# A graph network on one core: f32 tables split into three bfloat16 parts by ScalarE and VectorE in turns

## What is computed

```python
src = jnp.concatenate([_s, _d, _loop]); dst = jnp.concatenate([_d, _s, _loop])   # 103125 edges

# layer 0: attention with a bias by edge type
scores = jnp.sum(q[dst] * (k[src] + rel_bias), axis=-1) / SCALE
...
out = jax.ops.segment_sum(attn[:, :, None] * v[src], dst, num_segments=n)

# layer 1: three times
h = (x @ W).reshape(n, H, D)
e = jax.nn.leaky_relu(e_src[src] + e_dst[dst], NEG_SLOPE)
alpha = w / (denom[dst] + 1e-16)                     # w = exp(e - max)
out = jax.ops.segment_sum(h[src] * alpha[:, :, None], dst, num_segments=n)
```

## Time and profile before

| | us |
|---|---|
| runs | 8020.83, 8024.5, 8024.66 |
| median | 8024.5 |
| profiled execution | 8015.14 |
| its span | 8013.4 |

### The profile page before, as it was taken

How to read it: one execution, slowest core, us unless ns; L and a number is a source line. 1 busy time by engine, 2 the same in 40 slices (tenths; PEclk the granted TensorE clock), 3 DMA queues, 4 the chain that set the end, 5 groups by cost and what they waited for, 6 DMA issues and landing times. The chain is left out here.

```text
span 8013.4 us, 112882 instructions
## 1 busy us (share of the span) xinstructions
PE 2909.3 (36%) x28649; PEld 2368.4 (30%) x28650; DVE 4677.0 (58%) x10839; ACT 1435.1 (18%) x3773; POOL 3668.7 (46%) x4402
## 2 busy tenths in 40 slices
PE   4189633455555523344223432345200000001344
PEld 3168512344444422243223431334200000000122
DVE  9677345566666646687567764677544444444333
ACT  0123100111111112222112221344311111110000
POOL 0155224443333324565445544544466666563655
PEclk9999986676777766677566765666655555555677
DMA  0034223344434423345334443334332231222334
GB/s 21 10 92 108 58 75 96 96 105 101 101 88 96 92 59 70 80 83 77 67 75 83 84 69 64 77 74 73 53 51 51 52 52 51 49 51 55 77 83 80
DMA packets 293996, 576.70 MB, mean 72 GB/s; under 512 B 137262, under 2 KB 182043, under 8 KB 273827
## 3 DMA queue, kind: packets, MB, share of 16 engines
q0 software_dynamic: 113232, 255.82, 21.2%
q1 hardware_dynamic: 142642, 278.18, 11.3%
q10 hardware_dynamic: 38049, 41.86, 1.7%
HBM read 479.10 MB, written 29.32 MB: 63 GB/s over the span
## 5 line engine op out<-in xcount | busy, mean ns | idle before, releaser
L2992 PE MATMUL bank<-tab,oh 128*128 128x136 bf16 x11700 | 906.9, 251 | 704.3 <-PEq L2984 383.6
L2992 PEld LDWEIGHTS bank<-tab,oh 128*128 128x128 bf16 x11700 | 876.7, 113 | 765.2 <-issue 765.2
L1422 PE MATMUL bank<-ident,hid 128*128 128x128 f32 x125 | 55.8, 446 | 2622.7 <-PEq L1421 1482.1
L1422 PEld LDWEIGHTS bank<-ident,hid 128*128 128x128 f32 x125 | 22.7, 181 | 2669.4 <-issue 2669.4
L2735 POOL DMA_INDIRECT land_a<-table,idx_a x624 | 653.5, 1047 | 228.4 <-issue 166.4
L2754 POOL DMA_INDIRECT land_r<-table,idx_r x492 | 507.5, 1031 | 215.5 <-issue 148.4
L2915 ACT ACTIVATE rows<-bank 128x408 f32<-128x408 f32 x936 | 398.0, 514 | 848.6 <-ACTq L2914 640.2
L2841 DVE TENSOR_TENSOR prod<-prod 128x128 f32<-128x128 f32 (+4 forms) x621 | 536.5, 864 | 14.6
L2571 PE MATMUL bank<-tab_l,oh_l 128*128 128x128 bf16 x3846 | 407.5, 241 | 222.1 <-PEq L2534 102.0
L2827 DVE TENSOR_TENSOR prod<-rows,bank 128x5376 f32<-128x5376 f32 x75 | 431.6, 5755 | 61.1 <-DVEq L2826 30.5
L3218 PE MATMUL bank<-tab_l,oh_l 128*128 128x384 bf16 x1250 | 263.8, 381 | 454.9 <-PEq L3212 333.3
(11 more groups left out here) (515 smaller groups left out, 8530.2 us busy)
## 6 DMA issues: line engine op xcount, KB each, us to landing
loc<-el_loc SPq DMA_DIRECT2D x78, 1088.0 KB
loc_l<-el_loc SPq DMA_DIRECT2D x52, 1088.0 KB
typ_l<-el_typ SPq DMA_DIRECT2D x52, 672.0 KB
rows_r<-land_r SPq DMA_DIRECT2D x123, 272.0 KB
landings_l<-landings_l SPq DMA_DIRECT2D x41, 784.0 KB
attr<-in_edge_attr ACTq DMA_DIRECT2D x75, 343.8 KB
land_a<-table,idx_a POOLq DMA_INDIRECT x936
land_r<-table,idx_r POOLq DMA_INDIRECT x492
```

What stands on the lines that cost most here:

```text
L2992: last = pe.matmul(got[g % full][:, (c - of[0]) * W1:(c - of[0] + 1) * W1], oh[:, o], tab[:, t, x], start=n == 0, stop=n == len(parts) - 1 ...
```

## The change

The five steps of a group are divided. ScalarE makes the high part (`act_high`) and the middle part (`act_middle`) with activation copies; VectorE makes the two subtractions (`split_rest`, `split_low`), of which the second writes the low part straight as bfloat16, so the last cast goes. They hand on through `high_ready`, `rest_ready` and `middle_ready`. `rest` has two buffers, which in the attention and convolution passes lie in `kp` and `prod`, tensors that are unused at this time; `whole` has three. VectorE subtracts group g + 1 ahead of the low part of group g. ScalarE's order is the high parts of groups 0, 1, 2, the middle parts of 0 and 1, and then one high part (two groups ahead) and one middle part (one group ahead) at each step n.

In `l0_pass` ScalarE's `take_landed(0)` moves between step 3 and step 4. In `conv_pass` each step stands ahead of the copy of bank n. `sum_pass` gets a ScalarE program, with these copies alone. The diff, cut to one of three alike copies of each part (line numbers of the kernel before):

```diff
@@ -2089 @@  l0_pass
-            whole = [spare[:, k * BANKC * W0:...] for k in range(2)]
-            rest = spare[:, 2 * BANKC * W0:3 * BANKC * W0].rearrange("p (t w) -> p t w", w=W0)
+            whole = [spare[:, k * BANKC * W0:...] for k in range(3)]
+            rest = [kp[:].rearrange("p c w -> p (c w)")[:, k * BANKC * W0:...] for k in range(2)]
...
+            def act_high(act, g):
+                act.wait_ge(s(f"whole_in{g % 3}"), 16)
+                act.sem_inc(s(f"whole_in{g % 3}"), -16)
+                act.activation(tab_of(g)[:, :, 0], whole_of(g), ACT.Copy).then_inc(s("high_ready"), 1)
+
+            def act_middle(act, g):
+                act.wait_ge(s("rest_ready"), 1)
+                act.sem_inc(s("rest_ready"), -1)
+                act.activation(tab_of(g)[:, :, 1], rest_of(g), ACT.Copy).then_inc(s("middle_ready"), 1)
+
+            def act_split(act, n):
+                for g in range(n + 2 if n else 0, min(n + 3, len(tiles))):
+                    act_high(act, g)
+                for g in range(n + 1 if n else 0, min(n + 2, len(tiles))):
+                    act_middle(act, g)
...
-                        sp.wait_ge(s(f"whole_free{g % 2}"), 1)
+                        sp.wait_ge(s(f"whole_free{g % 3}"), 1)
...
-                    def split(g, m):
...
+                    def split_rest(g):
+                        dve.wait_ge(s("high_ready"), 1)
+                        dve.sem_inc(s("high_ready"), -1)
+                        dve.tensor_tensor(rest_of(g), whole_of(g), tab_of(g)[:, :, 0], ALU.subtract).then_inc(ch.semaphore, ch.one())
+                        dve.wait_ge(ch.semaphore, ch.count)
+                        dve.sem_inc(s("rest_ready"), 1)
+                        dve.sem_inc(s(f"whole_free{g % 3}"), 1)
+
+                    def split_low(g):
+                        dve.wait_ge(s("middle_ready"), 1)
+                        dve.sem_inc(s("middle_ready"), -1)
+                        dve.tensor_tensor(tab_of(g)[:, :, 2], rest_of(g), tab_of(g)[:, :, 1], ALU.subtract).then_inc(ch.semaphore, ch.one())
+                        dve.wait_ge(ch.semaphore, ch.count)
+                        dve.sem_inc(s("tab_ready"), 1)
+
+                    def split_table():
+                        split_rest(0)
+                        for g in range(len(tiles)):
+                            if g + 1 < len(tiles):
+                                split_rest(g + 1)
+                            split_low(g)
...
@@ -2506 @@  l0_pass, ScalarE
-                    take_landed(0)
+                    for n in range(len(tiles)):
+                        act_split(act, n)
+                        if n == 3:
+                            take_landed(0)
@@ -2910 @@  conv_pass, ScalarE
                         for g, of in enumerate(columns):
+                            if of_pass:
+                                act_split(act, g)
@@ -3197 @@  sum_pass
+                @block.scalar
+                def _(act):
+                    for n in range(len(sizes)):
+                        act_split(act, n)
```

More of the change, by code:

```diff
@@ L2126, in _ @@
                 def _(sp):
-                    for k in range(2):
+                    for k in range(3):
                         sp.sem_inc(s(f"whole_free{k}"), 1)
@@ L2874, in _ @@
                     onehots()
[L2875 to L2876 removed]
+                    split_table()
                     if number == 1:
@@ L3183, in _ @@
                     onehots()
-                    for g, m in enumerate(sizes):
-                        split(g, m)
+                    split_table()
                     chunks(0)
```

157 lines of the change are left out of this document (95 added, 62 removed).

## The result

Six executions of each kernel, side by side: after 7940.8 us (7926.2 to 7958.6), before 8017.2 (8006.5 to 8024.7). The ratio is 0.9906 with a 95% interval of 0.9891 to 0.9921, a gain of 76 us (63 to 87). The profiled execution took 7937.7 with a span of 7936.0, against 8013.4 before: 77.4 less.

A forecast was written before the change was run, and what follows sets the result against it. VectorE's split was taken as the path through five table-splitting stretches. Gains of 22 (attention), 10 and 10 (convolutions 2, 3), 4.3 (convolution 1) and 11.7 (last pass) sum to 58 us: 8024.5 - 58 = 7966.5, range 7942 to 8000.

The forecast's parts named there:

- Mechanism and bounds: Per group, VectorE's two subtractions bound attention (2.62 us) and the last pass (1.78), ScalarE's order the convolutions (2.17).
- The terms of the convolutions: Shorter split at the convolutions' starts: 4.3 us less in convolution 1, 10 us each in 2 and 3.
- the 0.5 for a late third load: Convolutions 2 and 3: estimated 0.5 us taken off the gain for the third load ahead of the first middle part.
- the tail: TensorE's last 78 products behind a convolution's split, 6.44 us, and the last copies: taken as the same.
- The last sum: Last pass: group 0 ends as now, then VectorE's 1.78 us a group; 11.7 us less, bounds 7 and 13.
- The attention pass: Its start: split stretch 24 us shorter, taken as 22 because TensorE may trail; bounds 17 and 24.
- I assume that this moves along unchanged: Attention pass, after loop entry: VectorE's wait of up to 7.86 us stays; 10 us either side in the range.
- Rival D: Slower: TensorE's instruction supply falls to about 0.4 us a product behind the splits in all passes; 8071 us, chance 0.04.
- so I let a pass end earlier by what its start gains: All five passes: later runs are chained to the start, so its gain carries to the pass's end; sum 58 us.
- Rival E: More gain: the stall behind attention's split shrinks, or TensorE gets the higher clock in the stretches; 7942 to 7950, chance 0.06.
- The base: Whole kernel: 8024.5 us, the median of three runs before the change, from which the 58 us were subtracted.

The follow-up runs named there:

- before_third: The kernel before, unchanged, run once more for its trace beside `after_again` and `own_late`: 8089.6 us.
- after_again: The changed kernel, unaltered, run once more beside the kernel before: 7995.7 us, ratio 0.9885.
- own_late: The changed kernel with convolution 1's load of its own rows issued behind the sixth table load instead of the second: 7997.8 us, ratio 0.9887.
- split_ahead: The changed kernel with ScalarE's split copies one step further ahead of its row copies in the convolutions: 7355.9 us, ratio 0.9906 to the kernel before.
- the second comparison: The kernel before, run beside a repeat of the changed kernel and kernels with the new split in only some passes: 8005.0 us.
- before_again: The kernel before, unchanged, run once more for its trace beside `split_ahead`: 7424.3 us.

## Why the prediction missed

**Mechanism and bounds: right.** VectorE's two steps bound the attention pass (2.58 a group, 2.62 forecast), ScalarE's order the convolutions (4.12 a pair, 4.34), VectorE the last sum (1.73 a group, 1.78). With three buffers the loads did not bound: ScalarE waited for one up to 1.3 us, in the attention pass and the last sum, and VectorE behind it did not. Convolution 1's first group waits for the load behind the own rows, as worked out: it was to end 17.98 us after the pass's start and ended at 18.15. ScalarE's copies of this kind, which no row of before had, take 0.54 for 408 columns and 0.86 for 792; 0.51 and 0.85 had been interpolated. A copy of 792 in the attention pass, and VectorE's wait in convolution 1:

```profile
1148.49 0.86 ACT L2129 ACTIVATE tab_l<-kp_l 128x792 bf16<-128x792 f32 x1 [0.35 <-ACTq L2128]
...
2874.03 0.58 DVE L2859 TENSOR_TENSOR tab<-prod,tab 128x408 bf16<-128x408 f32 x1 [6.55 <-DVEq L2858]
```

**The terms of the convolutions: too small.** First blocks at the 8000 level gain 6.9, 13.8 and 12.4 us on average over the traces, against 4.3, 10 and 10. Part is the loop: from group 0 to the last the forecast had 16.8 us, and 15.0, 15.0 and 15.3 were measured. Part is the start in convolutions 2 and 3, where the 0.5 for a late third load wasn't needed. The rest is the tail, TensorE's last products behind the split. I had it "the same", and it was shorter, at a higher granted clock. Convolution 2's tail before and after (windows from the last low part to the last product, columns as above):

```profile
3841.00:3848.40 7.40, 7.19 (x78) 7.06 (x78) 0.49 (x5) 1.53 (x4) 0.00 (x0) 0.64 0.00 0
...
3804.90:3810.40 5.50, 5.46 (x80) 5.14 (x78) 0.48 (x4) 1.98 (x4) 0.00 (x0) 0.88 0.00 0
```

The last 78 products take 7.4 us at a granted clock of 0.64, and 5.5 at 0.88. On average over the traces of the 8000 level the tail takes 0.9, 1.3 and 0.4 us less in the three convolutions. It is not the gathers: in every trace, before and after, ScalarE's copy of the landed rows starts 0.31 us behind TensorE's last product, so it never waits for a landing. Convolution 2 gives some back: its first to last block takes 789 to 793 us instead of 782 to 789, which stands in all kernels with the new split in the attention and convolution passes, also at the 7420 level (789.6 against 785.6). That I can't explain.

**The last sum** gains 12.6 us at the 7420 level and 13.5 on average at the other; 11.7 was forecast. Group 0 was done 2.4 us after the stretch's start, where the forecast had 3.1, as now, and the rest took 12.4 instead of 13.8.

**The attention pass: the stretch right, the step behind it wrong.** 22 was forecast for its start. The stretch gave 24.0, as worked out. At the 8000 level a third of that was lost behind it: VectorE's waits for TensorE's products in the first chunk add up to 12 to 15 us with the old split and to 21 to 24 with the new one (the longest was 7.86 and 12.85 us in the profiled pair), so that the first block gains 15.4 on average. "I assume that this moves along unchanged" is the sentence that failed. At the 7420 level 1.7 us of them are left with either split, and the gain is 23.6. Rival D's small pieces are there at one place, 63 products in 18.1 us or 0.29 a product; the profile shows only that TensorE waits for nothing else, and no run shows that the supply of its instructions is the cause. D was set aside because of the tail's 0.08 us a product, and that held (0.07 to 0.10 in the tails after). Nor does the stall go with the loop's entry, where the earlier trace rows have it: in the kernel after it lies ahead of the entry (pieces from 1159.76 on, bounds read at 1177.83), with no branch of TensorE from 1109.7 to its first piece, and at the 7420 level the same code has no stall (VectorE waits 1.68 us for its first product and not for the next five).

**The step that made the number wrong** is "so I let a pass end earlier by what its start gains", with the sum of the starts: what lies behind the starts was put at nothing. The starts measure 15.4 + 6.9 + 13.8 + 12.4 + 13.5 = 62.0 us, 4 over the forecast. That this comes so near is in part luck: the attention pass gave 6.6 less than its term and the other four 10.6 more. Behind the starts, convolution 3 gained 11 us more in the profiled pair and up to 40 in others, in a loop that the change doesn't touch: in the pair its 3715 products keep TensorE busy for 359 instead of 372 us, and in `before_third` for 397. The block of `before_third` at a granted clock of 0.65 takes 3.6 us more than its other one at 0.73; over the whole loop the clock is 0.67 in both of the pair and 0.65 in `before_third`. Why it falls otherwise there stays open. The 6.8 us of the edge pass are drift: `after_again` and `own_late` have 1572 and 1564 there, `before_third` 1561. Without the gain in convolution 3's loop and without the drift, at 7420, the change is worth some 61 us (66.2 by the traces with `split_ahead`'s edit, less an estimated 5 for that), close to the 58. Rival E, more gain by the clock or by a shorter wait behind the attention pass's stretch, was this case in part, and its size, 16 to 24 us over the forecast, holds the 18 that were measured. It had the place wrong: the clock in four of the five stretches is 0.50 as before, that wait grew (7.86 to 12.85 us), and the gain came behind the stretches, in the tails and in convolution 3's loop. It was given 0.06.

**The base.** The forecast took 8024.5 as the time before; the six executions beside the kernel after had 8017.2. Of the 25.7 us between forecast and measurement 7.3 are this, and 18.4 the gain's size. Counted from 8017.2 the range would have begun at 7934.7 and held the measured time: as a gain, 76 us lie inside it. The spread of three executions (4 us) was no measure of this kernel's: 23 of them, in the second comparison, go from 7972 to 8021.

## What to carry to other kernels

Where a stretch is bound by one engine's chain of small steps, count steps: dropping a cast by writing the subtraction into the narrow type gave 22 to 28 of some 61 us without a second engine, and of what the other engine's part gave, 13 to 15 us hung on the third buffer. When a second engine joins, write down the order of its program as a loop with everybody's steps in it; here that loop, not any engine's busy time, was the bound, and one step of look-ahead moved it (2.06 to 1.78 us a group). And before a sum of starts is trusted to 10 us, look how far two traces of the same kernel differ in the loops behind them.

## What the hardware showed beyond that

The same kernel runs at two levels 8 to 9% apart, 7424 and 8005 to 8090 us. It kept to one of them within each comparison, but 7424 and 8090 were measured on the same chip, some 40 minutes apart, so the level doesn't belong to the chip. Of the 678 us between the traces of `before_again` and `before_third` 392 are in the attention pass (1409 against 1802 us), 164 in the edge pass (1397 against 1561), 61 in the last sum and 40 in convolution 3. VectorE, ScalarE and GpSimd are busy for the same time to 1%, TensorE for 2840 against 2968 us. TensorE's groups in 200 us of the attention loop, `before_third` and then `before_again` (columns: busy us, mean ns, idle before and what ended it):

```profile
L2571 PE MATMUL bank<-tab_l,oh_l 128*128 128x128 bf16 x422 | 48.6, 252 | 24.9 <-issue 22.5 <-DVE kp_l L2328 1.2 <-PEq L2534 1.2
```

```profile
L2571 PE MATMUL bank<-tab_l,oh_l 128*128 128x128 bf16 x504 | 50.1, 238 | 6.3 <-PEq L2534 6.3
```

At the 8000 level 22.5 us in 200 pass in front of these products with nothing waited for ("issue"), at the 7420 level none are listed. VectorE's longest wait ahead of TensorE's first products goes the same way: 7.86 and 12.85 us in the profiled pair at the 8000 level, 1.68 in both traces of the other. What holds TensorE up there no run here shows, and what sets the level stays open.
